# First attention layer of a two-layer transformer block: eight runs of row-tiled products per batch made six

## What is computed

```python
x = x + L0_xattn(layernorm(x), ctx, ctx)      # 16 heads of 16 channels, softmax(q k^T / 4) v
x = x + L0_ffn(layernorm(x))                  # 8 experts, the best 2 of each token
x = x + L1_xattn(ctx, layernorm(x), ...)      # 16 heads again, with projections
x = x + L1_ffn(layernorm(x), ...)             # hidden width 1024, quantized
```

```python
q = layernorm(x)   # split in 16 heads, as k = v = ctx
scores = einsum('bhqd,bhkd->bhqk', q, k) / 4
out = einsum('bhqk,bhkd->bhqd', softmax(scores), v)
```

## Time and profile before

| | |
|---|---|
| runs, us | 1218.73, 1221.36, 1222.63 (median 1221.36) |
| profiled execution, span | 1218.4 us, granted TensorE clock 0.970; its time outside the span isn't listed apart |
| first attention layer | to about 260 us |
| TensorE busy, whole span | 1129.2 us (93%) |
| VectorE | 908.6 us (75%) |
| ScalarE | 743.3 us (61%) |
| GpSimd | 611.8 us (50%) |

### The profile page before, as it was taken

The page is one execution under the profiler, slowest core; times in us unless marked ns, Lnnn a source line. Parts: engine busy times, 40 slices in busy tenths (PEclk is TensorE's granted clock), DMA queues, the critical chain, the costliest instruction groups (busy, mean ns, idle before and its releaser), DMA issues. The chain is left out here.

```text
span 1218.4 us, 26789 instructions
## 1 busy us (share of the span) xinstructions
PE 1129.2 (93%) x9622; PEld 925.1 (76%) x9623; DVE 908.6 (75%) x1303; ACT 743.3 (61%) x983; POOL 611.8 (50%) x607
## 2 busy tenths in 40 slices
PE   3899999989899999999999999857999999999997
PEld 2566666679788999999999999745666666668886
DVE  7899999669488888878878777567888888743332
ACT  4687778856445555554555655365877887764442
POOL 3588777344686886722002000788877876002222
PEclk9999999989899999999999999956999999999999
DMA  6577766359936465523132111165656665402221
GB/s 216 202 254 249 268 237 227 132 201 355 325 127 195 142 190 167 174 100 113 43 112 69 34 52 43 55 229 185 216 196 217 208 229 183 155 28 70 69 69 35
DMA packets 121862, 194.19 MB, mean 159 GB/s; under 512 B 12208, under 2 KB 65456, under 8 KB 121648
## 3 DMA queue, kind: packets, MB, share of 16 engines
q1 hardware_dynamic: 105520, 148.57, 35.6%
q0 software_dynamic: 12656, 39.33, 10.3%
q10 hardware_dynamic: 3600, 5.12, 1.2%
HBM read 92.85 MB, written 51.12 MB: 118 GB/s over the span
## 5 line engine op out<-in xcount | busy, mean ns | idle before, releaser
L2389 PE MATMUL y_ps<-e_w,hiddenT_hi 128*128 x624 | 225.3, 403 | 1.9 <-DVE rows L2509 1.9
L2432 ACT ACTIVATE hidden<-hidden 128x1024 f32<-128x1024 f32 x78 | 82.8, 1062 | 190.6 <-DVE hidden L2470 168.1
L2372 PE MATMUL h_ps<-kvT_hi,tile_w_hi 128*128 128x256 f32 x624 | 179.2, 287 | 6.9 <-DVE kvT_lo L2492 6.9
L1673 DVE TENSOR_REDUCE neg_max<-big 128x4 fp32r<-128x1024 f32 x128 | 154.5, 1222 | 36.4 <-PE big L1397 33.8
L2372 PE MATMUL h_ps<-kvT_lo,tile_w_hi 128*128 128x256 f32 x624 | 178.5, 286 | 0.0
L2372 PE MATMUL h_ps<-kvT_hi,tile_w_lo 128*128 128x256 f32 x624 | 178.4, 286 | 0.0
L2390 PE MATMUL y_ps<-e_w,hiddenT_lo 128*128 x624 | 175.2, 281 | 0.0
L736 DVE TENSOR_REDUCE neg_max<-big 128x4 fp32r<-128x1024 f32 x128 | 155.1, 1217 | 23.3 <-PE big L485 22.0
L1567 ACT ACTIVATE probs<-big 128x1024 f32<-128x1024 f32 x128 | 130.7, 1023 | 46.2 <-PE big L1408 44.1
L644 ACT ACTIVATE probs<-big 128x1024 f32<-128x1024 f32 x128 | 130.6, 1022 | 44.3 <-PE big L496 44.2
L2498 DVE TENSOR_TENSOR hiddenT_lo<-hidden,hiddenT_hi 128x1024 fp32r<-128x1024 f32 x78 | 98.7, 1306 | 58.2 <-ACT hiddenT_hi L2443 53.7
(11 more groups left out here) (282 smaller groups left out, 2565.8 us busy)
## 6 DMA issues: line engine op xcount, KB each, us to landing
q_stack<-q_cut SPq DMA_DIRECT2D x96, 256.0 KB, 2.6
k_stack<-k_cut SPq DMA_DIRECT2D x72, 256.0 KB, 2.7
e_w<-in_L_ffn_w POOLq DMA_DIRECT2D x10, 1024.0 KB, 6.9
slots_out<-rows SPq DMA_DIRECT2D x39, 256.0 KB
slots_in<-rows POOLq DMA_DIRECT2D x37, 256.0 KB
slot_x<-slots_in SPq DMA_DIRECT2D x37, 256.0 KB
vals<-in_v_wide SPq DMA_DIRECT2D x16, 512.0 KB, 4.4
vals<-v_wide SPq DMA_DIRECT2D x16, 512.0 KB, 4.0
```

What stands on the lines that cost most here:

```text
L1673: nc.vector.tensor_reduce(neg_max[m % 2][:, :, :, g].rearrange("p q a -> p a q").bitcast(F32R), big[bank][:], AX.X, ALU.max, negate=True). ...
L2372: last = nc.tensor.matmul(h_ps[k][:, f % HF, :], w1[w][b.u][:, c, f * P:(f + 1) * P], xT[a][b.u][:, c, :], start=(n == 0), stop=(n == 3 * ...
L2389: nc.tensor.matmul(y_ps[q][:].rearrange("p s d -> p (s d)"), hT[0][o.u][:, f, rows], both, start=(f == 0), stop=False)
L2432: nc.scalar.activation(half(hidden, k), half(hidden, k), ACT.Gelu).then_inc(gelu_done, 1)
```

## The change

`AHEAD = (1, 5)` names two steps in which the score comes first. The maximum of step 1 moves ahead into step 0, behind its score, and that of step 5 into step 4. So the first row-tiled run of a batch becomes M0 S0 M1, and the score S1 joins M2 S2; likewise M4 S4 M5 and S5 M6 S6. What stood alone between the former runs is gathered: `logits` moves up behind pv3, and pv1 moves up behind `turn_neg` and `turn_norm2`. On ScalarE, pv1's copy moves along. The turn of the big and of the small banks does not change.

```diff
-    OUT_AT = 2
+    OUT_AT, AHEAD = 2, (1, 5)
...
+    def maxima_with(b, g):
+
+        return [maxima(b, k) for k in (g, g + 1) if (k == g) != (k in AHEAD)]
...
         for g in range(PAIRS):
-            m, gm = maxima(b, g)
-            big_order += [(name, t) for name, t in ((("max", gm), m), (("score", g), b), ("out" if g == OUT_AT else None, b - 1))
-                          if has(t) and name]
+            uses = [(("max", gm), m) for m, gm in maxima_with(b, g)]
+            uses.insert(0 if g in AHEAD else 1, (("score", g), b))
+            big_order += [(name, t) for name, t in (*uses, ("out" if g == OUT_AT else None, b - 1)) if has(t) and name]
...
                 for g in range(PAIRS):
-                    m, gm = maxima(b, g)
-                    if has(m):
-                        row_max(m, gm)
-                    if has(b):
+                    if g in AHEAD and has(b):
                         score(b, g)
+                    for m, gm in maxima_with(b, g):
+                        if has(m):
+                            row_max(m, gm)
+                        if g not in AHEAD and has(b) and (m, gm) == maxima(b, g):
+                            score(b, g)
                     if g == 0:
                         if has(b - 1):
                             pv(b - 1, 3)
-                    elif g == 1:
                         if has(b - 3):
                             logits(b - 3)
...
                         if b == BATCHES:
                             project_v(TAIL_KV)
-                    elif g == 5:
                         if has(b):
                             pv(b, 1)
...
                         if b == BATCHES:
                             kv_out(TAIL_KV)
+                        if has(b):
+                            pv_out(b, 1)
...
-                    elif g in (3, 5, 7):
+                    elif g in (3, 7):
```

## The result

| | before | changed |
|---|---|---|
| median of the runs, us | 1221.99 | 1233.76 |
| ratio, 95% interval | | 1.0103 (1.0084 to 1.0123) |
| profiled execution: time, span, us | span 1218.4 | 1237.02, 1235.3 |
| granted TensorE clock, whole span | 0.970 | 0.968 |
| last `att` of the first layer starts at, us | 253.2 | 266.1 |

The change makes the kernel slower by 1.0%: 11.8 us between the medians, 12.6 by the ratio. I forecast slower by 7.8 us, 1229.2, and a range up to 1232.5, so the direction was right and the size fell short by 4 to 5 us. The layer that was changed accounts for all of it: its last `att` stands 12.9 us later. The traced execution of the changed kernel is the slowest of its four (1229.7 to 1237.02), and 4 us more of its 16.9 us of span came behind the first layer, where no instruction was changed.

The account below looks back on a forecast made before the run. It took a loop of TensorE from S7 to M2 and VectorE from M2 to M6 as the bound. Terms 6.7 + 0.5 - 0.75 + 1.3 = +7.8 us on 1221.4 gave 1229.2 us, range 1224 to 1232.5.

Parts of the forecast that it names:

- What bounds the kernel: First attention layer: TensorE from S7 to M2, then VectorE from M2 to M6, close a loop of 13.87 us per batch.
- Its bank is not free.: "Out" reuses S1's bank and waits 0.76 us for S1's exponential, starting 1.66 behind S1.
- The period of 14.42: A batch of the first attention layer grows from 13.87 to 14.42 us, by 0.56.
- The two ways behind M3's reduction: To M6's reduction: VectorE's 5.03 us now, 4.88 if pv1's hold does not bind; TensorE's by pv1 5.02.
- The sum of 7.8: Whole first attention layer: 6.7 + 0.5 - 0.75 + 1.3 = +7.8 us.
- Start and end: Batches 1 and 2 gain 0.37 each, -0.75 us; batches 14 and 15 cost +0.99 and +0.34.
- Together ... +7.8 us: The step adding steady batches, lighter batches, start and end of the first attention layer to +7.8 us.
- More: Rival: ScalarE falls behind, S7's exponential starts late and M1 slips 0.3 in 12 batches, +3.6: 1232.8; chance 0.13.
- Faster: Rival: "out" is not held and TensorE's way to M2 counts: 1219, or 1216.5 with four boundaries saved; chance 0.08.
- Same: Rival: the late "out" is partly made up, 0.26 per batch, and the end costs nothing: about 1224; chance 0.12.

Follow-up runs that it names:

- the first gather alone: The changed kernel with pv1 and its copy back behind S5, so only M1 and logits move; ratio 1.0062.
- the second alone: The changed kernel with logits and M1 back in their old places, so M5 and pv1 still move; ratio 1.0011.
- "out" filled: The changed kernel with the products of S2 issued four times over in batches 3 to 14, ahead of "out"; ratio 1.0064.
- pv1's wait filled: The changed kernel with the transposes of norm2 issued twice, ahead of pv1; ratio 1.0106.
- logits beside "out": The changed kernel with logits moved from behind pv3 to between S2 and "out"; ratio 1.0038.
- the version that won: The kernel before with M1 moved into the first run and S6 put ahead of M6; ratio 0.9958, 1214.5 us.

## Why the prediction fell short

- **What bounds the kernel.** Right: the loop of TensorE up to M2 and VectorE from M2 to M6. Taking one wait out of it shortens the period (13.71, 13.54), putting one in lengthens it.
- **"Its bank is not free."** Right, to 0.05: "out" 1.71 behind S1 for a forecast 1.66, held 0.73 for 0.76, twelve times, from batch 3 to 14; the reciprocal waits on TensorE; in batch 2 a wait of 0.16.
- **The period of 14.42.** Measured 14.45. The two ways behind M3's reduction were sized right as well: 14.30 with the first gather alone, where VectorE's way binds (8.12 + 4.88 + 1.28 = 14.28), and 13.87 with the second alone.
- **The sum of 7.8.** Right in total for what it counts, and in part by errors that cancel. With "out" filled, so that the clock stays full, the last `att` stands at 261.0 against 253.2, +7.8, and the ratio is 1.0064, which is 7.8 us of 1220. By terms, from the same trace: batches 3 to 14 take 173.73 for 166.03, +7.7 for a forecast of 6.7 + 0.5; the start gains 1.04 (`att` at 64.85 for 65.89) for 0.75; the end costs 1.16 (22.47 for 21.31) for 1.33.
- **Start and end** in the changed kernel itself: up to the `att` at 64.55 it gains 1.34, of which 0.34 in the batch before that `att`; the end took 1.23 for 1.33 (243.57 to 266.11 against 231.92 to 253.23). The same `att` stands anywhere from 64.46 to 65.14 in the six traces with both gathers, so 0.75 and 1.04 can hardly be told apart.
- **The step that failed** is "Together ... +7.8 us", which prices every product at the durations of the earlier trace rows and so takes TensorE's clock as given. It held at 1.00 in the layer before, and I didn't ask whether it would with the new wait. In the trace it fell four times, +5.3 us; 7.8 + 5.3 = 13.1 for the 12.9 at the last `att`, and with the wait filled the ratio drops from 1.0105 to 1.0064 on the same chip.
- **Rivals.** "More" came nearest to the time (1232.8) by a mechanism that isn't there: M1 follows S0 at 0.24 and isn't held. "Faster" and "Same" both rested on an "out" that is free or made up later; neither is.

Shown: that the wait ahead of "out" makes the period longer, and that without TensorE's idleness in it the slow stretches are gone, with the same work around it (fill it and none is left in three traces, and on one chip the ratio falls from 1.0105 to 1.0064; fill the one ahead of pv1 and the time does not fall).

Not shown: whether the length of this one wait decides or all of TensorE's idle time in a batch. In an undisturbed batch TensorE is idle 1.57 us in the changed kernel (4 and 3 stretches in its two traces), 1.22 with the first gather alone (1), 1.12 with pv1's wait filled (1), 1.14 with logits beside "out" (none), 0.85 with "out" filled (none) and 0.57 in the kernel before (none). So both readings are left. A long wait by itself does not do it: in the kernel before S2 waited 0.85 in batch 1 and again in batch 2, and the granted clock stayed at 1.00. Open as well: why only some of the twelve equal waits bring a stretch, and where the kernel with pv1's wait filled spends the rest of its time.

## What to carry to other kernels

When a product is moved across others, count what is left between the producer of a bank and its next user, not only the boundaries saved: here, of four boundaries saved, two came back inside the gathered products; S2 ended 0.2 us earlier per batch for it, and 1.1 us of cover for an exponential was lost (1.99 us of work between S1 and "out" before, 0.90 after). A new wait on a matrix engine that was idle for only 0.57 of 13.86 us can have a second price, its clock; if a wait can't be avoided, repeating products inside it shows in one run how much of the loss is clock. And moving M1 alone, which uses the same spare room without uncovering anything, was part of the version that won.

## What the runs showed of the hardware

The granted clock fell from 2.4 to 1.2 GHz for about 3.4 us inside a layer where TensorE is busy about 89% of the time (12.88 of 14.45 us, as the profile counts it), during transposes that had waited 0.73 us. It did so too where pv1's wait of 0.57 was filled or not there. Waits of 0.57 in every batch without the one of 0.73 brought no fall, nor did two waits of 0.85 in the kernel before. Three of the falls came in the same batches in two traced executions of the changed kernel. From the start of a value product to the next product of another shape it is 1.00 us, whether that is a row-tiled pass or logits, in both kernels (131.43 to 132.43, 133.34 to 134.34). Where the shape stays the same the next starts sooner: from logits to "out" 0.91 us (91.02 to 91.93, logits beside "out"), for 0.99 from logits to a row-tiled pass (134.34 to 135.33).
